# Layer 1 attention on one Trainium2 core: packs of two float32r parts in both 64-row halves of the array, and the value product between the second and third score

## The reference, cut to what matters

```python
q = x @ W_q
latent_kv = (x @ W_k + x @ W_v) @ W_down_kv
k_rec, v_rec = latent_kv @ W_up_k, latent_kv @ W_up_v        # heads of 8
scores = einsum('bhqd,bhkd->bhqk', qh, k_rec) / sqrt(128)
scores = scores * exp(-0.01 * |t - t'|)
out = einsum('bhqk,bhkd->bhqd', softmax(scores), v_rec) @ W_o
```

## Time and profile before

| | |
|---|---|
| three runs | 1562.11, 1570.79, 1572.23 us (median 1570.79) |
| profiled execution | 1561.7 us, of which the profile's span is 1559.6 us |
| PE busy over the span | 1334.3 us (86%) |
| DVE, ACT, POOL busy | 1128.4, 906.1, 474.1 us |
| mean granted TensorE clock | 0.917 of full speed |

### The profile page before, as it was taken

The page is one execution under the profiler, slowest core; times in us unless marked ns, Lnnn a source line. Parts: engine busy times, 40 slices in busy tenths (PEclk is TensorE's granted clock), DMA queues, the critical chain, the costliest instruction groups (busy, mean ns, idle before and its releaser), DMA issues. The chain is left out here.

```text
span 1559.6 us, 23543 instructions
## 1 busy us (share of the span) xinstructions
PE 1334.3 (86%) x7952; PEld 751.4 (48%) x7952; DVE 1128.4 (72%) x1737; ACT 906.1 (58%) x1496; POOL 474.1 (30%) x986
## 2 busy tenths in 40 slices
PE   4298988619999999999754989999999979999998
PEld 1133333407877778777321222222222225777776
DVE  4366674377999999998547766888888243778885
ACT  3288885105555555555330766787887802767774
POOL 3255453003343343343220233223442301212210
PEclk8599999859999999999855898999999968999999
DMA  5524420015666666663347556665563040022110
GB/s 139 107 56 88 80 61 8 3 41 127 151 150 147 151 155 140 157 148 72 123 96 92 72 128 123 102 106 87 88 98 49 15 157 3 26 97 82 61 49 27
DMA packets 71415, 142.57 MB, mean 91 GB/s; under 512 B 11815, under 2 KB 44648, under 8 KB 64392
## 3 DMA queue, kind: packets, MB, share of 16 engines
q1 hardware_dynamic: 70660, 140.62, 41.3%
q10 hardware_dynamic: 648, 0.59, 0.1%
HBM read 124.20 MB, written 16.71 MB: 90 GB/s over the span
## 5 line engine op out<-in xcount | busy, mean ns | idle before, releaser
L1385 DVE CUSTOM_DVE_ANT_0 a_junk<-a_mring,a_COR 128x1024 bf16<-128x1024 f32 x256 | 304.8, 1222 | 90.0 <-PE a_mring L1286 89.8
L1373 ACT ACTIVATE a_PR<-a_ring 128x512 f32<-128x512 f32 x576 | 300.7, 603 | 118.7 <-PE a_ring L1317 118.6
L1260 POOL TENSOR_SCALAR_AFFINE_SELECT a_PR<-a_PR 128x128 f32<-128x128 f32 x512 | 134.6, 293 | 304.0 <-ACT a_PR L1373 303.8
L803 ACT ACTIVATE e_HH<-e_H 128x512 fp32r<-128x512 f32 x184 | 116.4, 633 | 162.5 <-DVE e_H L851 161.8
L1317 PE MATMUL a_ring<-a_QP,a_KP 74*128 74x512 bf16 (+3 forms) x768 | 181.2, 341 | 13.1 <-issue 5.7
L402 DVE TENSOR_SCALAR a_PR<-a_PR,a_lo,a_hi 128x1024 f32<-128x1024 f32 (+1 forms) x160 | 122.1, 774 | 77.1 <-ACT a_PR L376 74.4
L376 ACT ACTIVATE a_PR<-a_ring,a_ng 128x1024 f32<-128x1024 f32 (+1 forms) x160 | 155.0, 1033 | 13.3 <-PE a_ring L305 12.5
L1336 PE MATMUL a_OUT<-a_PR,a_V 128*9 128x512 f32 (+3 forms) x1536 | 154.7, 500 | 0.0
L822 DVE TENSOR_TENSOR e_HL<-e_H,e_HH 128x512 fp32r<-128x512 f32 x138 | 140.3, 1017 | 13.2
L1317 PEld LDWEIGHTS a_ring<-a_QP,a_KP 74*128 74x128 bf16 x768 | 57.9, 99 | 172.4 <-ACT a_PR L1373 119.6
L1676 DVE TENSOR_TENSOR e_HL<-e_GL,e_HH 128x512 fp32r<-128x512 f32 x144 | 109.2, 763 | 37.6 <-ACT e_HH L1644 34.1
(11 more groups left out here) (232 smaller groups left out, 2344.8 us busy)
## 6 DMA issues: line engine op xcount, KB each, us to landing
e_ROUTE<-routing SPq DMA_DIRECT2D x24, 704.0 KB
a_QP<-q_parts SPq DMA_DIRECT2D x72, 192.0 KB
e_RAW<-in_w_chunks SPq DMA_DIRECT2D x46, 192.0 KB, 7.5
a_QM<-q_parts SPq DMA_DIRECT2D x64, 128.0 KB, 5.4
e_GATE<-gates SPq DMA_DIRECT2D x8, 1024.0 KB, 4.7
e_ROUTE<-routing SPq DMA_DIRECT2D x8, 640.0 KB
a_KP<-k_parts SPq DMA_DIRECT2D x24, 192.0 KB
e_ROUTE<-routing SPq DMA_DIRECT2D x8, 576.0 KB
```

What stands on the lines that cost most here:

```text
L803: nc.scalar.activation(HH[n % NH][:], HT[n % NH][:], ACT.Copy).then_inc(high_done, 1)
L1260: last = nc.gpsimd.affine_select(out=d, in_=d, compare_op=keep, fill=0.0, base=0, pattern=[[step, P]], channel_multiplier=-step)
L1373: nc.scalar.activation(PR[g % NPR][:, j, :], ring[n % NRING][:], ACT.Exp).then_inc(s_read, 1)
L1385: nc.vector.tensor_tensor_reduce(out=junk[:, i % 2, :], in0=mring[k % 2][:], in1=COR[:, c:c + S], scale=1.0, scalar=-3.0e38, op0=ALU.mult, ...
```

## The change

- Packs hold **two float32r parts** in place of three bf16 ones (and of the separate two-part bf16 packs for the maxima). One pair of packs serves both the maxima and the scores: 34 rows (2 x 2 x 8, and the two rows of maxima), heads 0 and 1 of a quad in array rows 0 to 33, heads 2 and 3 in rows 64 to 97.
- A max tile no longer uses two strips at once; all its pieces are in the rows of its head. Instead the pieces of a max tile are written **between the pieces of two scores whose heads lie in the other 64 rows**. `MAX_ORDER` and `unit_head` see to that.
- `weigh` stands **between the first two and the last two scores** of a group.
- The third part is gone with its work on ACT, DVE and POOL. `values` and its copies move to the start of attention, the copies from DVE to ACT, three products a bank. PR, the buffer of exponentials, is allotted earlier and lends its space to decays and latent.
- The ones rows of K come from POOL memsets in place of a DMA. In the maxima the two rows of Q must be zero, so POOL clears them (two memsets a half).
- PE runs filler products (`keep_busy`, 2 after each of the 22 leading max tiles and 12 more before the first group) whose results nobody reads.
- Only the parts of the first 4 heads of sequence 0 are stored in the projection. ACT stores those of the other 12 at the start of attention; 16 stores for sequence 1 are spread over halves 1 to 4. A load brings 4 DMAs a half (queries) and 6 an iteration (keys).

The diff, cut:

```diff
 def project_l1
-                def second_part(g, w):
-                    act.wait_ge(rest_done, g * NV + w + 1)
-                    nc.scalar.activation(part(g, w, 1), rest[:, w, g % 2], ACT.Copy).then_inc(part2, 1)
+                def high(g, w):
+                    act.wait_ge(val_done, g * NV + w + 1)
+                    nc.scalar.activation(parts[:, w, 0, grp(g)], val[:, w, g % 2], ACT.Copy).then_inc(high_done, 1)
...
-                                values((g - 1) * PAIR_FILLS + 1)
...
+                            nc.vector.tensor_tensor(parts[:, w - 1, 1, grp(g)], val[:, w - 1, g % 2], parts[:, w - 1, 0, grp(g)].bitcast(F32),
+                                                    ALU.subtract).then_inc(low_done, 1)
...
+                act.wait_ge(first_stored, 2 * NV * 2 * 16)
+                packs.load_k(act, 0)
 class Packs
+        self.Q = [sb(f"a1_QP{s}", [HROWS + NROWS + 2, 2, 2, 2, GW], F32R) for s in range(2)]
+        self.K = [sb(f"a1_KP{s}", [HROWS + NROWS + 2, 2, 2, S], F32R) for s in range(2)]
...
+    def clear(self, h, done):
+        for pair in range(2):
+            rows = slice(pair * HROWS + NROWS, pair * HROWS + NROWS + 2)
+            self.nc.gpsimd.memset(self.Q[h // 2 % 2][rows, h % 2].rearrange("r h a t -> r (h a t)").bitcast(F32), 0.0).then_inc(done, 1)
 def attention_l1, SyncE
+                    if h % 2 == 0 and 1 <= it < NIT - 1:
+                        sp.wait_ge(s_read, h * UNITS)
+                        packs.load_k(sp, it + 1)
+                        packs.load_q(sp, h + 3)
 def attention_l1, TensorE
+                def max_piece(m, a, b, var):
...
+                    rows = slice(j // 2 * HROWS, j // 2 * HROWS + NROWS + 2)
...
+                    last = nc.tensor.matmul(mring[k % 2][:, a:b], QP[s][rows, h % 2, j % 2, var, row * P:(row + 1) * P],
+                                            KP[s][rows, j % 2, var, a:b], start=True, stop=True)
...
+                def group(g):
...
+                    score_half(g, 0)
+                    if g >= LAG:
+                        weigh(g - LAG)
+                    score_half(g, 1)
+
+                def score_half(g, two):
+
+                    tiles = range(issued(g - 1) if g else LEAD, issued(g))
+                    parts_of_unit = list(segments(g % NT, g // NT % 2))
+                    scores = [(n, *piece) for n in (2 * two, 2 * two + 1) for piece in parts_of_unit]
+                    maxima = max_pieces(tiles[two]) if two < len(tiles) else []
+                    for x in range(max(len(scores), len(maxima))):
+                        if x < len(scores):
+                            score_piece(g, *scores[x])
+                        if x < len(maxima):
+                            max_piece(tiles[two], *maxima[x])
...
+                for f in range(NFILL):
+                    values(f)
                 pe.wait_ge(cor_loaded, 32)
-                pe.wait_ge(out_clear, 1)
                 for m in range(LEAD):
                     if m == tiles_until_turn(0):
                         turn(0)
-                    max_tile(m)
+                    for piece in max_pieces(m):
+                        max_piece(m, *piece)
+                    if m == 0:
+                        pe.wait_ge(v_kept, NFILL)
+                    for n in range(2):
+                        keep_busy(n)
+                for n in range(12):
+                    keep_busy(n)
+                pe.wait_ge(out_clear, 1)
                 for g in range(NGROUP + LAG):
                     if g < NGROUP:
-                        for j in range(HQ - 1):
-                            scores(g, j)
-                        maxima(g)
-                        scores(g, HQ - 1)
-                    if g >= LAG:
+                        group(g)
+                    else:
                         weigh(g - LAG)
```

More of the change, by code:

```diff
@@ L38 @@
 NPART = 3
+PARTS1 = 2
 PAIRS = NPART * NPART * HD
@@ new lines, in __init__, with store @@
+        self.Q = [sb(f"a1_QP{s}", [HROWS + NROWS + 2, 2, 2, 2, GW], F32R) for s in range(2)]
+        self.K = [sb(f"a1_KP{s}", [HROWS + NROWS + 2, 2, 2, S], F32R) for s in range(2)]
+        self.q_loaded = [[sem(f"q_loaded{s}{half}") for half in range(2)] for s in range(2)]
+        self.k_loaded = [sem(f"k_loaded{s}") for s in range(2)]
+    def store(self, eng, g, w, i, h0, h1, done):
+        tok = slice(g * GW, (g + 1) * GW)
+        eng.dma_start((self.QS if w < 2 else self.KS)[h0:h1, w % 2, i, :, tok], self.parts[h0 * HD:h1 * HD, w, i, tok].bitcast(F32))\
+            .then_inc(done, 16)
@@ L1107, in attention_l1 @@
+def attention_l1(nc, t, packs, consts, OD):
     NT = KB + 1
@@ L1247, in _, with clear @@
                 store(NHALF - 1)
-                sp.wait_ge(out_stored, NHALF * 16)
+                for half in range(2):
+                    sp.wait_ge(out_stored[half], NIT * 16)
             @block.gpsimd
             def _(pool):
-                for g in range(NGROUP):
-                    T, half = g % NT, g // NT % 2
+                def clear(h):
+                    packs.clear(h, cleared)
+                    pool.wait_ge(cleared, (h - 1) * 2)
+                for h in (2, 3):
+                    clear(h)
@@ L1254, in _ @@
+                for g in range(NGROUP):
+                    T, h = g % NT, g // NT
+                    half = h % 2
+                    if 1 <= h < NHALF - 3 and T == (1 if half else KB // 2 + 1):
+                        pool.wait_ge(s_read, h * UNITS)
+                        pool.wait_ge(masked, masked_groups(g - 1) * HQ)
+                        clear(h + 3)
                     for j in range(HQ):
@@ new lines, in score_piece @@
+                def score_piece(g, n, a, b, kb, var):
+                    h, T, u, j = g // NT, g % NT, g * HQ + n, unit_head(g, n)
+                    s, a, b = h // 2 % 2, a - h % 2 * GW, b - h % 2 * GW
+                    rows = slice(j // 2 * HROWS, j // 2 * HROWS + NROWS + 2)
+                    if a == 0:
+                        if T == 0 and n == 0:
+                            pe.wait_ge(m_rows, (h + 1) * 64)
+                        if u >= NRING:
+                            pe.wait_ge(s_read, u - NRING + 1)
+                    last = nc.tensor.matmul(ring[u % NRING][:, a:b], KP[s][rows, j % 2, var, kb * P:(kb + 1) * P],
+                                            QP[s][rows, h % 2, j % 2, var, a:b], start=True, stop=True)
+                    if b == GW:
+                        last.then_inc(s_filled, 1)
```

368 lines of the change are left out of this document (147 added, 221 removed).

## The result

The changed kernel takes **1789.34 us** (median of 4 runs, 1788.38 to 1798.71), the kernel before 1566.81 in the same comparison (4 runs). The ratio is 1.143, 95% interval 1.137 to 1.149: 14% slower, where I had forecast 1504 us and given slower 8 in 100. The profiled execution took 1788.38 us, its span 1786.5.

The account below looks back on a forecast made before the run. PE was taken to set the pace. Copy intervals -39.2, first 11 groups -6.7 and start -16 sum to -62 from the profiled 1561.7, giving 1499.7; with 4.5 towards the median, 1504 us, range 1466 to 1558.

Parts of the forecast that it names:

- the groups then start at full clock: First 11 groups: fillers keep PE busy in the lead, so groups begin at clock 1.0.
- the clock falling after such a wait: Attention, sign of being wrong: the clock drops after PE waits for key packs at the sixth group of even halves.
- Half = 21.7 us: Attention's halves: each takes 21.7 us in place of 23.9.
- 2 x 0.60: Group with two max tiles: each half group takes 0.60 us, its weight loads passing one door in line.
- 0.8 taken: Each half of attention: today's 0.9 us of idle PE stays, counted as 0.8.
- Value product in the middle removes most of the 0.3: Each group: value product between score pairs removes most of the 0.32 us for which ACT starves.
- I count the lead even: Leading max tiles before the first group: fillers lose 0.6 us a tile until the clock rises, then fit; no net change.
- First 11 groups, -6.7: Start of attention's groups: 26.5 us in place of 33.2, a gain of 6.7.
- first max tile at 810: Projection and start: without third parts, the first max tile comes at 810 against 826.4, -16 us (-8 to -24).
- 6 us in all: Attention's pack loads: new waits for the second iteration's packs and for key packs cost 6 us, between 0 and 25.
- Rival B: Half group: pieces wait for their own weight loads, 0.73 us in place of 0.60; 1538 or 1519 us; chance 0.15.
- Rival C: Score and max products: the array's 64-row halves don't stream at once; halves 26.0 us or more, 1569 to 1606; chance 0.11.

Follow-up runs that it names:

- kernel 1: The changed kernel with its packs padded by zero rows, so that scores and max products run over 64 rows in place of 34: 1589.22 us.
- kernel 4: The kernel before the change, with its score products over the first 34 of their 74 rows: 1791.71 us.
- kernel 2: The changed kernel with parts, packs and negated maxima in bfloat16 in place of float32r, 34 rows kept: 1648.11 us.
- kernel 12: The kernel before the change, with only its value product split in two column halves, after the second and fourth scores: 1664.45 us (median of 4).
- kernel 9: kernel 5 with the value product cut in two column halves, one behind each pair of scores: 1545.38 us.
- kernel 5: kernel 1 without the 56 filler products ahead of the first group: 1574.89 us.
- kernel 6: kernel 1 with the value product behind the fourth score: 1577.03 us.
- kernel 11: kernel 5 with both bfloat16 parts and the value product cut in two column halves: 1496.68 us (median of 4), ratio to the kernel before 0.9545.
- kernel 8: kernel 1 with each max tile in the same 64 rows as the scores around it, so nothing can run side by side: 1641.33 us.
- kernel 7: kernel 1 with all maxima ahead of the fourth score and the value product last: 1573.56 us.
- kernel 10: kernel 5 with bfloat16 parts in place of float32r, still over 64 rows: 1525.79 us.

## Why the prediction was wrong

- **The step that failed** is the one that I never took: every term assumed full clock ("the groups then start at full clock", "clock 1.0 from the first group"). I looked for idle time as the only thing that could lower it ("the clock falling after such a wait"), and counted the fillers as protection. Kernels 1 and 4 show the cause from both sides: over 34 rows the clock is 1.2 GHz with PE 99 to 100% busy, over 64 rows, zeros included, 2.4. (Rows are not all that counts: by kernels 2 and 12, the type and the order have a part in it.) Its price: first to last copy 575.5 us here, 386.4 in kernel 1 (889.4 to 1275.8), so 189 of the 209.7. The Trainium skill ("TensorE: Matmul & The Clock Gate", What's actually happening) says that the gate goes by how busy PE has been; by that rule this kernel would have kept 2.4 GHz, and the trace disagrees (115.94 of 116.80 us busy at 0.50).
- **"Half = 21.7 us"** would have been wrong at full clock as well: 25.3 and 26.4 or more (kernel 1). Two terms were mis-sized. The half group, "2 x 0.60", measures 0.66 for whole pieces (kernel 9); I had the four-byte loads pass one door in line, but the two halves' loads start together (both at 971.22). And of waits the sum had only "0.8 taken" for idle PE, where kernel 1 has 2.1 us a half (10.3 in 127.0): I called PE's work the bound and didn't follow the loop through the three-bank ring. Splitting the value product gives back 1.3 us a half (25.3 to 24.0, kernels 5 and 9) in float32r and 1.5 in bfloat16 (23.2 to 21.7). Group by group, 2.60 stands against my 2.28: 0.12 of it are the two pairs, 0.18 what the split takes away (2.42 in kernel 9). Groups with one max tile, for which I had 2.14, are no shorter (none in kernel 1 under 2.58).
- **"Value product in the middle removes most of the 0.3"**: false, 24.9 with it last against 25.3 (kernel 6). I had seen ACT's 0.32, and I had written that four scores stand between two value products in either order, but did not draw from it that the place then can't matter.
- **"I count the lead even"**: wrong by 27.3 us here. The figure of 0.6 us a tile until the clock rises was right in kind (a max tile took 2.1 us against my 1.8), but it rose only for the last 0.5 us of the lead. Over 64 rows, too, the fillers cost 14 us (kernel 5).
- **First 11 groups, -6.7**: +10.8; with the clock mostly up about nothing (kernel 1: 31.5, kernel 5: 34.0, against 33.2). Only kernel 11 comes near, with 27.3.
- **Start, "first max tile at 810", -16**: right, 805.2 and -21.3. Its cause as I gave it (the third parts gone) was not tested alone.
- **New waits, "6 us in all"**: within its bounds of 0 and 25, if they are what lengthens the even halves. Those of kernel 9 exceed the odd ones by 12.7 us in sum, twice my figure, those of kernel 11, with half the bytes, by 4.4.
- **Rival B** (loads not hidden) was half right at full clock: a pair takes 0.66, between my 0.60 and B's 0.73. **Rival C** (halves not at once) is refuted by kernel 8, where they really don't overlap and a half takes 28.1 us. My 8 in 100 for slower lay on C, so the right direction would have come from a wrong reason.

In kernel 11 the sum holds: first to last copy 324.7 us, where I had 326.6; all in all 63.5 less than before in span, where I had 62. That it fits is partly luck: kernel 11 is another kernel than the one forecast, with the two errors (four-byte type, uncut value product) and the fillers taken out. It also keeps only 16 bits of each value.

Open: how much of the clock's behaviour is the type's (34 rows of bfloat16 keep either level, 34 of float32r only the low one, but for 3.4 us behind the fillers), and how near to the edge 64 rows are: in the one profiled execution of each, kernels 1, 5 to 7 and 9 to 11 left 2.4 GHz in attention for 3.4 to 10.2 us at a time and came back, kernel 8 for up to 23.9, and the four executions of kernel 11 lie within 0.5%, which is all that is known. Why cutting the value product lost kernel 12 its clock over 74 rows, and not kernels 9 and 11 theirs over 64, is open too.

## What to carry to other kernels

Before packing products into fewer rows, find in the profile a stretch with as few rows, and read its granted clock; if there is none, fill the rows up with zeros: they cost no PE time (kernels 2 and 10, in bfloat16). Where a ring is shorter than the number of tiles between two long products, follow the loop through the consumer and cut the long product in pieces that cover its waits, before moving it. And read a product that the change left alone (here the value product, 500 to 831 ns): it tells a slower clock from more work in one line.

## What the runs showed of the hardware

- A TensorE busy for 315.90 of 315.90 us stayed at 1.2 GHz, with scores over 34 rows and maxima over 32; with the scores over 74 the same program runs at 2.4 (1.00 over 119.50 us). Zero rows count as rows (kernel 1).
- In kernels 2 and 12 both levels hold themselves: each shows stretches of 100 us and more at either, in one execution and with the same instructions.
- Two float32r products of 64 rows each, in different halves of the array, start in the same 10 ns, and so do their weight loads (kernel 9, 971.22); at full clock a half without this takes 1.8 to 2.8 us more (kernel 8).
- At half clock a half took 38.9 us, not twice the 26.1 of kernel 1 (889.4 to 1255.3, 14 halves): waits that lie open at 2.4 GHz (PE idle for 10.3 of 127.0 us, kernel 1) are covered at 1.2 (0.9 of 116.8).
